# Filler matmuls on TensorE in the idle spans of four stages of a graph kernel on one core

## What is computed

```python
x = norm(x + L0(x))      # mean over neighbours, two dense layers
x = norm(x + L1(x))      # attention over edges, then two dense layers
x = norm(x + L2(x))      # weighted sum over neighbours
x = norm(x + L3(x))      # messages by relation, forward and backward

# L1, the scores of an edge:
alpha = einsum("ehc,ehc->eh", q[dst], k[src] + e) / sqrt(C)
# L3, last of its layers only:
ht    = einsum("ne,reh->rnh", x, weights[-1])
out   = segment_sum(ht[type, src] + b[type], dst) + segment_sum(ht[type + 9, dst] + b[type + 9], src)
```

## Time and profile before

| | us |
|---|---|
| median of 3 runs | 5429.41 (5418.67 to 5431.08) |
| the profiled execution | 5436.53 |
| its span, first to last instruction | 5434.8 |
| mean granted TensorE clock | 0.694 |
| busy: TensorE 56%, VectorE 41%, ScalarE 11%, GpSimd 63% | |

### The profile page before, as it was taken

The page is one execution under the profiler, slowest core; times in us unless marked ns, Lnnn a source line. Parts: engine busy times, 40 slices in busy tenths (PEclk is TensorE's granted clock), DMA queues, the critical chain, the costliest instruction groups (busy, mean ns, idle before and its releaser), DMA issues. The chain is left out here.

```text
span 5434.8 us, 50013 instructions
## 1 busy us (share of the span) xinstructions
PE 3062.4 (56%) x13750; PEld 2237.6 (41%) x13751; DVE 2231.2 (41%) x2709; ACT 614.3 (11%) x1076; POOL 3413.0 (63%) x3213
## 2 busy tenths in 40 slices
PE   3899989567777777744918633343333333333333
PEld 1788879233333333324917422232222323232223
DVE  7999985445555454568901331111111111101112
ACT  0455540000000000004701000000000000000000
POOL 2888868466556555657770356666666666666664
PEclk7999999666666666657958766665665656555555
DMA  5566667144444444425825332222222111111111
GB/s 177 157 181 192 177 198 230 37 131 138 132 133 139 132 135 130 139 87 159 259 62 195 136 100 70 69 64 60 60 59 60 48 46 46 45 46 46 46 46 46
DMA packets 498663, 599.91 MB, mean 110 GB/s; under 512 B 190115, under 2 KB 367441, under 8 KB 496248
## 3 DMA queue, kind: packets, MB, share of 16 engines
q0 software_dynamic: 117856, 246.12, 16.5%
q1 hardware_dynamic: 337751, 229.77, 14.8%
q10 hardware_dynamic: 42944, 122.68, 6.0%
HBM read 406.69 MB, written 204.36 MB: 112 GB/s over the span
## 5 line engine op out<-in xcount | busy, mean ns | idle before, releaser
L720 POOL DMA_INDIRECT rec_by_src<-rec,pos x782 | 1123.3, 1436 | 524.6 <-issue 238.9
L1132 PE MATMUL ps<-g_got,g_hot 128*128 x3224 | 687.5, 367 | 1225.8 <-issue 797.4
L1132 PEld LDWEIGHTS ps<-g_got,g_hot 128*128 128x128 f32 x3224 | 605.7, 272 | 1320.2 <-issue 1318.9
L1592 POOL DMA_INDIRECT sc_kv<-kv,d_src x806 | 761.8, 945 | 533.9 <-DVE sc_kve L1644 260.2
L1032 POOL DMA_INDIRECT g_got<-y_forward,d_msg x782 | 739.3, 945 | 381.8 <-issue 230.1
L1032 POOL DMA_INDIRECT g_got<-y_back,s_msg x782 | 737.8, 943 | 381.2 <-issue 233.5
L805 PE MATMUL ps<-ln_low,ln_hot 128*125 128x256 f32 x2848 | 620.3, 381 | 20.3 <-DVE ln_low L782 16.1
L805 PEld LDWEIGHTS ps<-ln_low,ln_hot 128*125 128x125 f32 x2848 | 535.6, 188 | 104.8 <-issue 24.4
L1043 DVE TENSOR_TENSOR g_hot<-ps,src_loc 128x1024 f32<-128x1024 f32 x101 | 120.6, 1221 | 992.5 <-remote 450.4
L1699 PE MATMUL ps<-w_e,sc_attrT 128*128 128x512 f32 x404 | 320.0, 887 | 246.0 <-ACT sc_attrT L1611 216.3
L1051 DVE TENSOR_TENSOR g_y<-ps,ms_b 128x384 f32<-128x384 f32 x75 | 41.8, 558 | 808.8 <-remote 474.2
(11 more groups left out here) (323 smaller groups left out, 3283.7 us busy)
## 6 DMA issues: line engine op xcount, KB each, us to landing
linked<-ln_out SPq DMA_DIRECT2D x320, 224.0 KB
ve<-sc_kve ACTq DMA_DIRECT2D x202, 256.0 KB
wv_ve<-ve SPq DMA_DIRECT2D x101, 512.0 KB
l_links<-linked SPq DMA_DIRECT2D x25, 800.0 KB
l_links<-linked ACTq DMA_DIRECT2D x25, 800.0 KB
f_links<-linked SPq DMA_DIRECT2D x25, 800.0 KB
f_links<-linked ACTq DMA_DIRECT2D x25, 800.0 KB
attr_pairs<-ln_feats POOLq DMA_DIRECT2D x7, 2048.0 KB
```

Of the source, the lines that this page charges most:

```text
L720: pool.indirect_dma_start(out=dram["rec_by_src"], out_offset=bass.IndirectOffsetOnAxis(ap=S["pos"][:, c:c + 1], axis=0), in_=S["rec"][:, c ...
L1132: last = pe.matmul(ps[:, bass.ds(columns[j], width)], hot[:, q, j, :], got[:, bass.ds(slots[j], width)], start=False, stop=True, skip_grou ...
L1592: pool.indirect_dma_start(out=kv[:, q, j, :], out_offset=None, in_=dram["kv"], in_offset=bass.IndirectOffsetOnAxis(ap=S["d_src"][:, c:c + ...
```

## The change

TensorE gets matmuls of a block of zeros (`nil`, bf16, set to zero by VectorE at the block's start) with itself, which I call fillers here:

- scores: 8 of 512 columns before each spread matmul (L1682), behind its waits, written to the same place, which the spread matmul then overwrites;
- second node layer: 8 of 384 columns behind each of the six steps of the first two chunks, into the spare part of bank 6; the wait for VectorE's `cleared` moves from behind these steps to before the first fillers;
- g3: 44 of 384 columns behind each group, 30 behind those with `rows_of` beside them, added onto the spare part of bank 6, which VectorE clears first;
- g4: 44 behind each of the 96 groups of the loop, none in the last five.

```diff
+        nil = m.sb(tag + "_nil", [P, 3 * P], BF16)
+        spare = ps[:, 6 * BANK + P:7 * BANK]
+        KEPT_BUSY, KEPT_BUSY_BESIDE = 44, 30
...
+            dve.memset(nil[:, :], 0.0).then_inc(emptied, 1)
+            dve.memset(spare, 0.0).then_inc(emptied, 1)
             if fresh:
                 dve.memset(ps[:, 0:BLOCKS * D], 0.0).then_inc(cleared, 1)
...
+            pe.wait_ge(emptied, 2)
             if fresh:
                 pe.wait_ge(cleared, 1)
+
+            def keep_busy(times):
+                for _ in range(times):
+                    pe.matmul(spare, nil[:, 0:P], nil[:, :], start=False, stop=True, skip_group_check=True)
...
                     landed_group(i, k, lands_in(n), size(n))
+                    keep_busy(KEPT_BUSY_BESIDE if n in beside else KEPT_BUSY)
...
                     for k in range(RING):
                         landed_group(i, k, GROUP)
+                        keep_busy(KEPT_BUSY)
...
+    KEPT_BUSY = 8
...
+            def keep_busy(times):
+                for _ in range(times):
+                    pe.matmul(spare, nil[:, 0:P], nil[:, :], start=True, stop=True)
+
             steps = (turn, widen, narrow)
             for c in range(2):
                 for step in steps:
                     step(c)
-            pe.wait_ge(cleared, 1)
+                    if c == 0 and step == turn:
+                        pe.wait_ge(emptied, 1)
+                        pe.wait_ge(cleared, 1)
+                    keep_busy(KEPT_BUSY)
...
+        nil = m.sb("sc_nil", [P, STEP * P], BF16)
+        KEPT_BUSY = 8
...
                 before_last(pe, heated, q, i)
+                for _ in range(KEPT_BUSY):
+                    pe.matmul(spread_loc(q), nil[:, 0:P], nil[:, :], start=True, stop=True)
                 pe.matmul(spread_loc(q), S["ones"][0:1, :], locr[0:1, q, :], start=True, stop=True).then_inc(spread[q], 1)
```

More of the change, by code:

```diff
@@ L938, in gather_sum @@
         hot = m.sb(tag + "_hot", [P, WAYS, GROUP, P])
+        nil = m.sb(tag + "_nil", [P, 3 * P], BF16)
+        emptied = m.sem(tag + "_emptied")
         landed = [m.sem(f"{tag}_landed{q}") for q in range(RING)]
@@ L1331, in mlp_and_linked_sum @@
         ps, half = S["ps"], ROWS // 2
+        nil, spare, emptied = m.sb("f_nil", [P, 3 * P], BF16), ps[:, 6 * BANK + P:7 * BANK], m.sem("f_emptied")
         w1, w2 = S["w_l1"][:, 0, :], S["w_l1"][:, 1, :]
@@ L1557, in scores @@
         spread = [m.sem(f"sc_spread{h}") for h in range(WAYS)]
-        cleared = m.sem("sc_cleared")
+        cleared, emptied = m.sem("sc_cleared"), m.sem("sc_emptied")
+        nil = m.sb("sc_nil", [P, STEP * P], BF16)
+        KEPT_BUSY = 8
         ps = S["ps"]
```

## The result

| us | before | changed |
|---|---|---|
| median, same chip | 5430.24 (5418.67 to 5443.68, 4 runs) | 6033.12 (5994.05 to 6048.8, 4 runs) |
| ratio | | 1.110, 95% interval 1.104 to 1.116 |
| profiled execution, its span | 5436.53, 5434.8 | 5994.05, 5992.3 |
| mean granted clock | 0.694 | 0.851 |

The account below looks back on a forecast made before the run. GpSimd's gathers, 1.25 us each when free, were thought held up by TensorE's crawls. Scores -235, first sum net -118, second -133, node layer -64 and memsets +2 gave -548, hence 4880 us, range 4790 to 5200.

Parts of the forecast that it names:

- the one from TensorE's rests to the crawls: Crawls, stretches with TensorE passes some 2.8 us apart, come from its rests; fillers end them; chance 0.68.
- the floor of 1.25 us a gather: Scores and both sums: a GpSimd that never waits starts a gather each 1.25 us: 1006, 985 and 976 us.
- the scores (-235): With eight fillers a TensorE step takes 5.09 us, about level with GpSimd's 5.0; the stage gets 235 us shorter.
- the sums (-144, -133): Both gather sums: GpSimd runs at its own pace; the first 144 us less, the second 133 with its end.
- the node layer: Second node layer: 127 us less without crawls; the cure was trusted half, so 64 us less.
- Rival 2: Fillers make TensorE the bound; loss if high-level share is under 0.76 (sums), 0.71 (scores); about 6085 us; chance 0.09.
- This state undoes itself: Argument against TensorE becoming the bound: where it works throughout, its granted clock is 0.98 to 1.00.
- Rival 4: The clock gate is faulty: crawls come at their own times and stall fillers too; about 6400 us; chance 0.02.
- Rival 3: Nothing that counts: crawls have another cause and stay, a higher clock makes up for fillers; 5430 us; chance 0.03.
- rival 1: Half a cure: crawls also come in nearly dense work and cost more each; 5155 us, 5010 to 5350; chance 0.18.
- Price of a filler: On TensorE at the high level, 0.22 us for 512 columns and 0.165 for 384; the low level doubles them.
- End of the first sum: Fillers behind each of the last four groups delay the next block by 26 us.

Follow-up runs that it names:

- group 4: Follow-up runs sharing one chip with crawls, where the kernel before took 5419.62 us and the changed kernel 5949.93 us.
- the run of group 4 with pauses: The changed kernel with a 128x256 GpSimd memset behind each gather of the two sums alone: 5750.72 us, 1.062.
- the paced pair of group 3: Kernel before and changed kernel, both with GpSimd memsets behind gathers of scores and sums and node layer scatters: 5299.2 us without fillers, 5332.26 with.
- group 3: Four follow-up runs sharing one chip, without crawls, where the kernel before took 4657.65 us.

## Why the prediction was wrong

- **The step that failed** is the one from TensorE's rests to the crawls: that keeping it busy would end them. The prediction said of it "What ties them to idleness is correlation" and still gave it 0.68. With it fell the floor of 1.25 us a gather that the terms of the scores (-235) and the sums (-144, -133) rest on. What the runs showed in its place: crawls come where GpSimd issues indirect DMAs faster than one each 1.42 us or so. With TensorE resting as much as before, 27 of 97 raises were on time at a spacing of 1.25 and 97 of 97 at 1.44. Resting and crawling went together because the same stages have GpSimd at its free pace; the node layer, dense and crawling from the first, was the counterexample that I saw and weighed at a half. The floor is right on the chip without crawls. On the others it is 1.42 in the sums, and in the scores, where a gather of twice the bytes took 1.58 (1271 / 805, and 1.58 again at a spacing of 1.34), probably something like it; no run paced the scores alone on a chip with crawls.
- **Why a loss and not a zero.** TensorE's slack is what let a crawl pass: 3.8 us of work in GpSimd's 11.3 a group. Fillers took it. The second sum with 0, 12 and 44 of them, all on the chip of group 4: 1108.3, 1125.7, 1237.9 us. The crawls now hold up 60 instructions a group instead of 16 passes, and the 0.9 us that are free per group don't catch up. How much of the loss is the slack, and how much that fillers themselves make completions later (the run of group 4 with pauses), is not separated.
- **Rivals.** Rival 2's point was a high level for under 76% of the time in the sums and 71% in the scores; it was 70% in all three. By its formula a sum's group would take 18.3 - 9.2 x 0.70 = 11.9 us (measured 1230.6 / 97.6 = 12.6) and a scores step 6.36 (7.2): +56 of the +125 us in the second sum, but only +14 of the +184 in the scores. Its 6085 us lie near 6033 by luck, since they take h = 0.5. "This state undoes itself" failed, since crawls end a stretch of high clock too. Rival 4 had half of the mechanism, stalls whatever TensorE does, but not at their own times, and overpriced it: 6400 instead of 6033. Its 0.02 was far too little, with GpSimd's row beside it. Rival 3 had the crawls' cause elsewhere, rightly, and wrongly took the fillers to be paid for by the clock; rival 1 had rightly that a crawl costs more without slack, and still counted on half a cure.
- **Price of a filler: right.** Eight of 512 columns in the scores at the high level, up to the spread pass:

```profile
1519.09 1.02 PE L1727 MATMUL ps<-w_e,sc_attrT 128*128 128x512 f32 x2
1519.95 1.89 PE L1709 MATMUL ps<-sc_nil 128*128 128x512 bf16 x8
1521.77 0.69 PE L1710 MATMUL ps<-sc_locr,ones 1*128 1x512 f32 x1
```

  1.82 us for eight (1519.95 to 1521.77), 0.23 each against 0.22. A step is 4.79 us (1514.30 to 1519.09) against 5.09. In the sums 37 took 6.18 us, 0.167.
- **End of the first sum:** +26 forecast, +27 without crawls; +55 with them (4635.1 to 4703.1, 68 us against 13.4).
- **Node layer:** the 127 us of a whole cure are there (124 by pacing, 140 by moving the scatters), the cure was another. The fillers gave +8, and the layer's matmuls took 293 us as before.

## What to carry to other kernels

A wait that ends late on one engine may be made by what another engine issues: before curing the waiting engine, compare a healthy and a sick stage for every engine, and the semaphores' times against the ends of records. Busy work pays only where the clock is the bound (in the paced pair of group 3 it was not: 0.57 and 0.94 gave the same 1126 us); it takes away the slack that hides other stalls, so try a few of it first. A free-running issue pace seen between waits is not yet a pace that a stage can keep: divide the stage by its count as well. Where completions come late, try indirect DMAs further apart (here 1.44 us or more) beside TensorE's work, and compare on the same chip: on one chip of five the same pauses only cost time.

## What the hardware showed beyond that, and what stays open

The kernel before took 5412 to 5439 us in four groups and 4658 in one, on separate chips, the same code and data; some 770 us are a property of the chip or of what stood around it. Besides the time, late completions give it away, and missing records: the very same program (the kernel before with paced scatters) left 78,145 semaphore changes in the trace on the chip of group 3 and 33,761 on that of group 4. Each gather raises its semaphore 16 times; in the second sum 16.0 of these are recorded on the chip without crawls, 2.7 in the kernel before on the first, 14.4 with GpSimd paced at 1.44 and 15.7 at 1.66. So records go missing on the chips with crawls, and in this stage most where GpSimd issues fastest. Where the 1.42 us are spent is open: the DMA packets of the gathers go on at GpSimd's pace during a crawl (256 for 8 gathers, 4750 to 4760 as 4730 to 4740), the DMA share is 0.18, VectorE's and ScalarE's completions are late as well, and a DMA of 64 rows counts like one of 128. All runs were recorded by the profiler, so the crawls, and the 1.42 us with them, may be made by the recording itself. That rival is untested, and the missing records make it a serious one. The Trainium skill says of the notification block that its inner pipeline holds producers back rather than lose a record (NOTIFIC — the notification-queue block, "Overflow: three behaviours, one of which stalls the engine"); no run here shows it, and no run without the profiler was made. What the change does on a chip without crawls was not measured; the nearest is the pair of group 3, +33 us.
